# Half of the context values' projection and write moved behind the attention output projection, and both block-diagonal spreadings behind x1, in a fused decoder layer

## The reference

```
x = layernorm(x + self_attention(x))          # 16 heads of 64, over the 128 tokens of a sequence
x = layernorm(x + cross_attention(x, ctx))
x = layernorm(x + ffn(x))

# cross attention: within ONE token, over its 16 heads
q, k, v = (x @ Wq.T + bq, ctx @ Wk.T + bk, ctx @ Wv.T + bv), each reshaped to (b, s, 16 heads, 64)
scores = einsum('bshd,bsgd->bshg', q, k) / 8
out    = einsum('bshg,bsgd->bshd', softmax(scores), v)
out    = transpose(out, (0, 2, 1, 3)).reshape(b, -1, 1024) @ Wo.T + bo

# ffn: a light and a heavy branch, each gelu(rms_norm(x) @ w1 + b1) @ w2 + b2; all tokens take both
```

## Time and profile before

| what | value |
|---|---|
| median of 3 runs | 486.5 us (483.74, 486.5, 489.27) |
| the profiled execution | 491.25 us |
| its span in the trace | 489.4 us |
| TensorE busy | 426.4 us, 87% |
| VectorE busy | 342.6 us, 70% |
| ScalarE busy | 242.7 us, 50% |
| GpSimd busy | 146.5 us, 30% |
| mean granted clock of TensorE | 0.972 |

### The profile page before, as it was taken

How to read it: one execution, slowest core, us unless ns; L and a number is a source line. 1 busy time by engine, 2 the same in 40 slices (tenths; PEclk the granted TensorE clock), 3 DMA queues, 4 the chain that set the end, 5 groups by cost and what they waited for, 6 DMA issues and landing times.

```text
span 489.4 us, 12635 instructions
## 1 busy us (share of the span) xinstructions
PE 426.4 (87%) x4788; PEld 364.3 (74%) x4788; DVE 342.6 (70%) x751; ACT 242.7 (50%) x828; POOL 146.5 (30%) x218
## 2 busy tenths in 40 slices
PE   8779699999898977999898977899898989999793
PEld 7568577778787866778787866778787877778683
DVE  2543788884958794884958794875958798967534
ACT  3584646534565353534565353643565364645431
POOL 5030425050330533050321542151321543512121
PEclk9889899999999997999999997999999999999998
DMA  8800201110100112010100112010100110101002
GB/s 214 308 2 1 50 7 45 55 40 2 29 23 12 40 26 70 13 38 1 30 23 12 39 27 68 17 35 5 29 18 16 37 29 21 43 6 43 21 1 64
DMA packets 43588, 19.10 MB, mean 39 GB/s; under 512 B 36544, under 2 KB 40896, under 8 KB 43536
## 3 DMA queue, kind: packets, MB, share of 16 engines
q1 hardware_dynamic: 42688, 16.88, 12.5%
q0 software_dynamic: 560, 1.38, 1.1%
q10 hardware_dynamic: 288, 0.07, 0.1%
HBM read 8.88 MB, written 1.05 MB: 20 GB/s over the span
## 4 chain that ended last, share of the span: by engine, by line
PE 61%; DVE 21%; issue 9%; ACT 4%; POOL 3%; DMA 2%; SPq 0%; POOLq 0%; DVEq 0%; ACTq 0%
PE ps L1018 7%; PE ps L923 6%; PE ps L1096 6%; PE ps L1071 6%; PE ps L948 6%; DVE pt L660 4%; DVE qt L705 4%; PE ps L1196 3%; PE ps L903 3%; PE ps L972 3%; PE ps L905 3%; PE ps L1135 3%; PE ps L904 3%; DVE ot L643 3%; DVE neg_max L712 3%
## 5 line engine op out<-in xcount | busy, mean ns | idle before, releaser
L496 ACT ACTIVATE p<-ps,neg_max 128x128 f32<-128x128 f32 x256 | 91.1, 414 | 66.9 <-DVE neg_max L712 66.9
L386 POOL TENSOR_TENSOR p<-p,row_inv 128x1024 f32<-128x1024 f32 x32 | 60.4, 1898 | 104.1 <-DVE row_inv L794 97.1
L489 ACT ACTIVATE pt<-ps 128x512 f32<-128x512 f32 x64 | 34.9, 607 | 66.6 <-PE ps L1018 66.5
L496 ACT ACTIVATION_READ_ACCUMULATOR p<-ps,neg_max 128x1 f32 x256 | 65.3, 255 | 0.0
L705 DVE TENSOR_TENSOR qt<-ps,bq 64x256 f32<-64x256 f32 x128 | 53.4, 417 | 7.5 <-PE ps L1135 5.8
L1018 PE MATMUL ps<-ident,p 128*128 128x128 f32 x256 | 37.2, 300 | 10.3 <-issue 7.1
L712 DVE TENSOR_REDUCE neg_max<-ps 128x4 f32<-128x512 f32 x64 | 42.1, 683 | 0.2 <-PE ps L1122 0.2
L1018 PEld LDWEIGHTS ps<-ident,p 128*128 128x128 f32 x256 | 31.7, 154 | 13.8 <-issue 11.5
L1135 PE MATMUL ps<-x1t,wq 128*128 128x128 f32 x256 | 36.5, 286 | 5.8 <-DVE pt L660 3.0
L948 PE MATMUL ps<-wo,ot 128*128 128x128 f32 x256 | 32.3, 279 | 10.0 <-DVE ot L643 10.0
L1135 PEld LDWEIGHTS ps<-x1t,wq 128*128 128x128 f32 x256 | 31.1, 191 | 11.8 <-DVE pt L660 8.1
(11 more groups left out here) (138 smaller groups left out, 891.7 us busy)
## 6 DMA issues: line engine op xcount, KB each, us to landing
v<-v2s SPq DMA_DIRECT2D x256, 32.0 KB
xg<-x_t SPq DMA_DIRECT2D x4, 256.0 KB, 2.7
pt<-w_qk SPq DMA_DIRECT2D x4, 256.0 KB, 7.2
cg<-ctx_t SPq DMA_DIRECT2D x4, 256.0 KB, 3.1
wo<-w_o SPq DMA_DIRECT2D x2, 512.0 KB, 9.1
out<-x2b SPq DMA_DIRECT2D x4, 256.0 KB, 2.3
xres<-x_nat SPq DMA_DIRECT2D x15, 64.0 KB, 1.7
bv_row<-b_v POOLq DMA_DIRECT2D x1, 512.0 KB, 10.7
```

The costliest lines, as they stand in the source:

```text
L386: nc.gpsimd.tensor_tensor(ph, ph, row_inv[:, 8 * half:8 * half + 8].unsqueeze(2).to_broadcast([T, 8, T]), ALU.mult).then_inc(p_ready, 1)
L496: last = nc.scalar.activation(p[:, hd * T:(hd + 1) * T], bank(S_BANK[q])[:, pos * T:(pos + 1) * T], ACT.Exp, bias=neg_max[:, hd:hd + 1], a ...
```

## The change

On TensorE the second half of the context's values (three products) is issued behind the attention output projection instead of ahead of it. On VectorE the second half of their bias and write is issued behind the statistics of the first norm instead of ahead of the residual sum. On VectorE spreading 0 moves from ahead of maximum 0 to behind x1; spreading 1 stays behind maximum 1, and so both are behind x1. The waits go with their instructions.

```diff
--- before.py
+++ after.py
@@ -749,10 +749,13 @@
                     if d:
 
                         dve.wait_ge(v2_moved, 16 * 16 * (s - 1))
-                    for u in range(2):
+
+                    def values2(u):
                         dve.wait_ge(mm_v2, 2 * s - 2 + u + 1)
                         nc.vector.tensor_tensor(v2s[:, u * BANK:(u + 1) * BANK], bank(V2[u]),
                                                 bv2_row[:, u * BANK:(u + 1) * BANK], ALU.add).then_inc(v2s_ready, 1)
+
+                    values2(0)
                     dve.wait_ge(mm_o, s)
                     dve.wait_ge(xres_ready, s)
                     nc.vector.tensor_tensor(t1[:], bank(O, D), xres[b_par][:], ALU.add).then_inc(sum1_ready, 1)
@@ -762,15 +765,16 @@
                     dve.wait_ge(bq_scaled, 1)
                     dve.wait_ge(stats1_ready, s)
                     nc.vector.bn_aggr(mv1[:], st1[:]).then_inc(mv1_ready, 1)
+                    values2(1)
+                if a:
+                    score_max(0)
+                if bc:
+                    dve.wait_ge(rs1_ready, s)
+                    nc.vector.tensor_scalar(x1[:], t1[:], mv1[:, 0:1], rs1[:, 0:1], ALU.subtract, ALU.mult).then_inc(x1_ready, 1)
                 if d:
                     if static and s == 2:
                         dve.wait_ge(in_mask, 16)
                     block_diagonal(s, 0)
-                if a:
-                    score_max(0)
-                if bc:
-                    dve.wait_ge(rs1_ready, s)
-                    nc.vector.tensor_scalar(x1[:], t1[:], mv1[:, 0:1], rs1[:, 0:1], ALU.subtract, ALU.mult).then_inc(x1_ready, 1)
                 if a:
                     score_max(1)
                 if d:
@@ -1075,7 +1079,8 @@
                     if static and s == 1:
                         pe.wait_ge(w_lo, WV2_SPLIT)
                     own = slice((phase - 1) % GB * T, ((phase - 1) % GB + 1) * T)
-                    for u in range(2):
+
+                    def value2(u):
                         ring_wait(u)
                         cols = slice(u * BANK, (u + 1) * BANK)
                         if u == 0:
@@ -1083,6 +1088,8 @@
                         nc.tensor.matmul(bank(V2[u]), cg_lo[:, own], wv2_hi[:, cols], start=True, stop=False)
                         nc.tensor.matmul(bank(V2[u]), cg_hi[:, own], wv2_hi[:, cols], start=False, stop=False)
                         nc.tensor.matmul(bank(V2[u]), cg_hi[:, own], wv2_lo[:, cols], start=False, stop=True).then_inc(mm_v2, 1)
+
+                    value2(0)
                     if static and s == 1:
                         pe.wait_ge(in_wo, 16)
                     if late:
@@ -1096,6 +1103,7 @@
                         last = nc.tensor.matmul(bank(O, D), ot[:, c * T:(c + 1) * T], wo[:, c * D:(c + 1) * D],
                                                 start=c == 0, stop=c == NC - 1)
                     last.then_inc(mm_o, 1)
+                    value2(1)
                 if d:
                     ring_wait(3)
                     transpose_p2(s)
```

More of the change, by code:

```diff
@@ L773, in step @@
                     nc.vector.tensor_scalar(x1[:], t1[:], mv1[:, 0:1], rs1[:, 0:1], ALU.subtract, ALU.mult).then_inc(x1_ready, 1)
+                if d:
+                    if static and s == 2:
+                        dve.wait_ge(in_mask, 16)
+                    block_diagonal(s, 0)
                 if a:
```

## The result

The changed kernel takes 498.0 us (median of 4 runs, 494.36 to 500.6), against 487.88 us before on the same chips: a ratio of 1.0215, interval 1.0118 to 1.0312. A second measurement of the same kernel, in the experiments, gives 1.0185 (1.0147 to 1.0222). By these ratios it is 9 to 10 us slower; the forecast was 6.1 us, and 498.0 lies outside its range.

What follows compares the result with a forecast made beforehand. The prediction took TensorE and VectorE to hand the chain to each other, VectorE bounding most steps' second half. Step delays 2.9 + 1.2 + 0.3 + 0.8 + 0.1 + 0.8 = 6.1 us gave 492.6 us from 486.5, range 487.5 to 495.0.

Steps and rivals of the forecast that it cites:

- a step of this kind gets 0.58 us longer: Steps 2, 5, 9, 13, 15: spreading 1 and the query projection come 0.58 us later; 2.9 us together.
- 0.48 for step 14: Step 14: the statistics' late aggregation is taken up by the new idle time before maximum 0, leaving 0.48 us.
- 0.10 for 3, 7 and 11: Steps 3, 7, 11: VectorE's 0.48 us wait for ScalarE's split of x hides most of the delay; 0.10 us each.
- 0.27 for 12: Steps 4, 8, 12: ScalarE's copy, which held the query projection, comes earlier; about 0.27 us of delay left each.
- 0.8 for the last step: Step 16, without scores: weighted values 0 wait for spreading 0, now behind x1; 0.8 us.
- The wait for the first bank: Maximum 0 needs the first bank of scores, ready 1.19 us after the scores start, as read from step 1.
- Rival 2: Maximum 0 doesn't wait, its first bank being ready when the value write ends; 488.3 us, chance 0.10.
- rival 1: The four-step loop's jump swallows delays of steps 1 to 10 in its two pauses; 489.3 us, chance 0.10.
- Rival 3: The path through x1 decides the query projection's start, 0.51 us earlier in 15 steps; 478.8 us, chance 0.07.
- rival 4: TensorE's granted clock falls through a new 0.8 us hole, about 3 us per fall; 505 us, chance 0.04.
- holes of that size didn't take the clock down: Argument against the clock falling: the hole before x1's transposition, 0.86 us on average before, shrinks and had caused no fall.

Runs made afterwards that it cites:

- the other order of the scores: Changed kernel with the scores of a half issued bank by bank, four products of the first bank, then four of the second: 493.17 us, ratio 1.0125.
- one fill ahead of the weighted values: Changed kernel with one idle 128x384 product on TensorE ahead of weighted values 0, its result unread: 492.76 us, ratio 1.0095.
- the one with the early spreading: Kernel before, with spreading 0 ahead of the residual sum and its weights' transposition ahead of the output projection: 479.88 us, ratio 0.9838.
- the kernels with one product as fill: Changed kernel with one idle 128x384 product, ahead of weighted values 0 (492.76 us, 1.0095) or ahead of the query projection (493.23 us, 1.0113).

## Why the prediction was wrong

**The mechanism and the sum of the steps held.** The term "a step of this kind gets 0.58 us longer" measured 0.58, 0.63, 0.61 and 0.61 (steps 2, 5, 9, 13) and 0.51 in 15; 0.48 for step 14 measured 0.50 to 0.52 where no stretch was in it (the changed kernel's second profile, the other order of the scores, one fill ahead of the weighted values); 0.10 for 3, 7 and 11 measured 0.12, 0.08, 0.07; 0.27 for 12 measured 0.31; 0.8 for the last step 0.75. Taken from the run with one fill ahead of the weighted values, which has no stretch at half clock, with steps 6 and 10 only up to the jump (0.17 and 0.41), these differences add up to 6.0 us; 6.1 were forecast. The ratios of the three kernels without such stretches are 1.0095, 1.0113 and 1.0125, or 4.6 to 6.1 us; they were also 5 to 6 us less at half clock than the kernel before, so by the line through all runs they would be 6.9 to 7.0 us slower at its clock.

**The wait for the first bank** (1.19 us, read from one step) was right: 1.19 in step 9 of the changed kernel and of the one with the early spreading. Rival 2 fell by this.

**The jump swallowed nothing.** The two pauses without a releaser were 3.77 and 3.36 us before and 3.38 and 3.20 after (3.60 and 3.22 in the second profile), 6.5 and 6.6 us together in the kernels with one product as fill; rival 1 asks for 1.86 and 1.42 us less. What varies is the stretch at half clock that begins in each pause: 6.8 and 6.8 us in the profile before, 6.8 and 3.4 after. That is most of the −0.72 of step 10, where 0.41 more was due, and part of why runs of one kernel differ by 1%. The Trainium skill (Runtime: NRT & Kernel Launch, Instruction fetch mechanics) says that a taken branch out of the resident pages forces a fetch before execution can go on; that the delay is carried on through the jump agrees with it. Rival 1 fell.

**Rival 3 fell**: spreading 1 was last at line 1143 in 14 steps.

**The step that failed is rival 4**, its chance of 0.04 and the sentence "holes of that size didn't take the clock down", by which the forecast's sum has nothing for the clock. The clock did fall, beside the forecast mechanism and not in its place: 4 stretches of 0.7 to 0.9 us, 3.3 us. I had priced a fall at 3 us and thought of it as all or nothing; each was at half for only 3.4 us, and the hole ahead of the second output projection took 0.7 us of that. So the rival's own 505 us was wrong too.

The argument went by the largest single hole, which had been 0.85 us before and stays at 0.83. It also set 0.56 us ahead of the query projection beside it, which is the idle time of the weight loads; TensorE's own hole there was 0.32 us. But the change spread its holes over the second half of a step and made them more: 0.23, 0.83 and 0.54 us in step 9 instead of 0.85 and 0.32. Summed over the step that is 1.60 us of waiting where there had been 1.17, in more pieces. The three kernels that gave TensorE 0.6 to 0.8 us more to do in this part of the step, each at another place, have 0.88 to 1.06 us of these holes left in step 9; all lost the stretches and 3 to 5 us with them, while the same other order of the scores changed nothing in the kernel before. So the reason given for the chance of 0.04 did not hold. The sum of the holes is no rule either: the kernel before had 0.85 and 0.56 us in steps 4, 8 and 12, 1.41 us together, and kept its full clock there.

Two things stay open: why steps 4, 6, 8 and 10 or 14 have stretches and 5, 9 and 13, with the same holes, have not; and why the kernel with only spreading 0 moved has the same holes and but one stretch.

The two together, 6.0 and 3.3 us by the steps of the profiles, or 6.2 and 2.8 us by the clocks of all runs, are the 9 to 10 us measured.

## What to carry to other kernels

An operation on an engine that waits at two places is cover for one of the waits: ask which wait it covers now and which it will cover there, and put it into the longest one whose inputs can be had. Two moves in one change are worth two sums: here one of them cost 6.5 us by itself, and the other, nearly free by itself, seems to gain 1 to 3 us once the first has a better place. And when a change opens holes on TensorE, look at all holes of a step together and not at the longest, and give the clock a term of its own: its falls cost here about half as much again as the waits themselves.

## What the hardware showed

- TensorE's granted clock fell to half in stretches of about 3.4 us in which no single hole ahead was over 0.83 us, and in the profiles with one added product of 128x384 in a step, at either of two places, it stayed at full there. Over 139 runs each us at half clock went with 0.34 us more time.
- 32 passes of products with 64 rows took 2.06 us when they took the two halves of the rows, and two PSUM banks, in turns, and 2.82 us when four products on one half and one bank followed each other.
- The two pauses at the loop's jump were 9.1 us together in the profile of the kernel with six more products of 128x128 in a step, and 6.4 to 7.1 us in the eleven others.
